# Layer 0's output products moved within the sixteen slots of a batch, with a ring of 14 attention outputs

## The reference

```
latent = x @ Wkv_down                      # (b, 512, 64)
q = x @ Wq                                 # 16 heads of 64
k, v = latent @ Wk_up, latent @ Wv_up      # 16 heads of 64
attn = softmax(causal(q k^T / 8))
x = layernorm(x + einsum(attn v, Wout))
...
```

## Time and profile before

| what | value |
|---|---|
| time, median of 3 runs | 1711.63 us (1711.25 to 1713.56) |
| profiled execution: own time | 1704.8 us |
| profiled execution: span | 1702.8 us |
| PE busy share of the span | 93% |
| DVE, ACT, POOL | 71%, 60%, 28% |
| mean granted clock of PE | 0.975 |
| last matmul of layer 0's attention ends | 763.5 us into the span |

### The profile page before, as it was taken

The page is one execution under the profiler, slowest core; times in us unless marked ns, Lnnn a source line. Parts: engine busy times, 40 slices in busy tenths (PEclk is TensorE's granted clock), DMA queues, the critical chain, the costliest instruction groups (busy, mean ns, idle before and its releaser), DMA issues. The chain is left out here.

```text
span 1702.8 us, 29270 instructions
## 1 busy us (share of the span) xinstructions
PE 1584.4 (93%) x9060; PEld 1102.6 (65%) x9060; DVE 1213.1 (71%) x4130; ACT 1016.8 (60%) x2544; POOL 470.8 (28%) x853
## 2 busy tenths in 40 slices
PE   7999999999999999987799977899999998899996
PEld 5667676767676766753588845666666655376765
DVE  4888878887888878755655546999999886134445
ACT  3876767676766767634444454677777766634340
POOL 4001001010101010100275467677786643100001
PEclk9999999999999999998899977999999999999998
DMA  5111111111121211103055628677686665000000
GB/s 165 38 48 45 40 38 38 50 44 48 40 50 38 52 43 38 38 7 100 12 170 163 140 68 113 88 111 106 103 118 87 95 86 98 1 7 25 13 25 31
DMA packets 72583, 111.67 MB, mean 66 GB/s; under 512 B 13265, under 2 KB 38321, under 8 KB 72305
## 3 DMA queue, kind: packets, MB, share of 16 engines
q1 hardware_dynamic: 61024, 81.04, 24.3%
q0 software_dynamic: 10016, 26.48, 6.9%
q10 hardware_dynamic: 1392, 2.29, 0.4%
HBM read 40.04 MB, written 18.87 MB: 35 GB/s over the span
## 5 line engine op out<-in xcount | busy, mean ns | idle before, releaser
L394 ACT ACTIVATE c_probs<-c_probs,a_negmax 128x128 f32<-128x128 f32 (+3 forms) x512 | 280.5, 553 | 0.0
L399 ACT ACTIVATE c_probs<-a_ps_trans 128x512 f32<-128x512 f32 (+1 forms) x256 | 125.0, 488 | 213.0 <-PE a_ps_trans L300 212.1
L1885 ACT ACTIVATE c_probs<-a_ps_st 128x384 f32<-128x384 f32 (+1 forms) x384 | 191.1, 529 | 90.2 <-PE a_ps_st L1685 88.7
L2038 DVE CUSTOM_DVE_ANT_0 a_junk<-a_ps_score,c_mask 128x128 f32<-128x128 f32 (+3 forms) x512 | 220.1, 487 | 33.5 <-PE a_ps_score L1663 30.4
L472 DVE CUSTOM_DVE_ANT_0 c_probs<-a_ps_score,c_mask 128x128 f32<-128x128 f32 (+3 forms) x512 | 219.6, 486 | 15.2 <-PE a_ps_score L281 14.1
L300 PE MATMUL a_ps_trans<-c_ident,c_probs 128*128 128x128 f32 x1280 | 188.0, 277 | 17.6 <-DVE c_probs L489 15.9
L300 PEld LDWEIGHTS a_ps_trans<-c_ident,c_probs 128*128 128x128 f32 x1280 | 146.4, 141 | 87.9 <-issue 39.3
L575 POOL TENSOR_SCALAR a_rstd<-a_mv 128x4 f32<-128x4 f32 x8 | 1.8, 231 | 689.3 <-DVE a_mv L502 689.3
L280 PE MATMUL a_ps_score<-a_kh,a_qs 128*128 128x128 f32 (+3 forms) x512 | 167.2, 350 | 1.3 <-issue 1.1
L489 DVE TENSOR_SCALAR c_probs<-c_probs,a_recip 128x128 f32<-128x128 f32 (+3 forms) x512 | 164.4, 386 | 4.5
L1685 PE MATMUL a_ps_st<-a_qs,a_ks 128*128 128x512 f32 (+3 forms) x512 | 149.7, 362 | 16.7 <-ACT c_probs L1885 8.6
(11 more groups left out here) (290 smaller groups left out, 3157.2 us busy)
## 6 DMA issues: line engine op xcount, KB each, us to landing
a_qs<-a_qlow SPq DMA_DIRECT2D x128, 128.0 KB, 2.2
slot_out<-m_y SPq DMA_DIRECT2D x80, 128.0 KB, 2.0
a_qs<-a_words_even SPq DMA_DIRECT2D x64, 128.0 KB, 4.1
a_ks<-a_words_even SPq DMA_DIRECT2D x64, 128.0 KB, 5.5
c_X<-in_x SPq DMA_DIRECT2D x8, 512.0 KB, 3.9
token_rows<-c_X SPq DMA_DIRECT2D x8, 512.0 KB, 5.7
a_qs<-a_counts SPq DMA_DIRECT2D x32, 128.0 KB, 4.3
a_qs<-a_hid SPq DMA_DIRECT2D x32, 128.0 KB, 4.7
```

The costliest lines, as they stand in the source:

```text
L394: act.activation(at, at, ACT.Exp, scale=-1.0, bias=negmax[:, n % 4, i:i + 1], accum_out=rowsum[:, n % 4, i:i + 1]).then_inc(s_exp, 1)
L399: act.activation(probT[:, n % 4, TGCOL[grp]:TGCOL[grp] + TGLEN[grp]], ps_trans[(3 * n + grp) % 2][:, 0:TGLEN[grp]], ACT.Copy).then_inc(s_p ...
L1885: act.activation(probT[:, r8, col:col + width], ps_st[item % 2][:, 0:width], ACT.Exp).then_inc(s_stc, 1)
L2038: dve.tensor_tensor_reduce(out=junk[:, to:to + keys], in0=ps_score[g][:, at:at + keys], in1=C.mask[:, L - keys:L], scale=-1.0, scalar=3.0e ...
```

## The change

The output products of a batch go from steps 20, 22, 24, 26 to steps 20, 24, 30, 32, their additions with them, and the batch's `write` from step 28 to 36. Modulo 16 the products are then in 4, 8, 14 and 0, and `write` in 4. Since the last product of a batch comes six slots later, the ring `yT` gets 14 entries for 12. Its two new entries hold, until pairs 12 and 13 are written, the small weights that had tensors of their own; the sum of the memory is the same. Because `latent` of a batch now falls between the second and the third product of the batch two before, the waits around `ps_kv` are set anew.

```diff
-NY = 12
+NY = 14
...
-        wdq, wuqT = S.sb("wdq", [P, P]), S.sb("wuqT", [P, P])
-        wdkv, wukT, wuvT = S.sb("wdkv", [P, 2, P]), S.sb("wukT", [P, 2, P]), S.sb("wuvT", [P, 2, HD])
-        wkr, wqr = S.sb("wkr", [64, P]), S.sb("wqr", [64, P])
+        wuvT = S.sb("wuvT", [P, 2, HD])
...
+        spare = yT[:, NY - 2:NY, :].rearrange("p r t -> p (r t)")
+        wdq, wuqT = spare[:, 0:P], spare[:, P:2 * P]
+        wdkv, wukT = (spare[:, 2 * P * j:2 * P * (j + 1)].rearrange("p (c d) -> p c d", d=P) for j in (1, 2))
+        wkr, wqr = spare[0:64, 6 * P:7 * P], spare[0:64, 7 * P:8 * P]
...
-        START, KEYS, VALUES, KEEP_VALUES, OUT, ADD, WRITE = 12, 13, 2, 3, (20, 22, 24, 26), (21, 23, 25, 27), 28
+        START, KEYS, VALUES, KEEP_VALUES, OUT, ADD, WRITE = 12, 13, 2, 3, (20, 24, 30, 32), (21, 25, 31, 33), 36
...
                 def latent(b):
...
                     if b >= 2:
-                        pe.wait_ge(s_sum, TT * (b - 1))
+                        pe.wait_ge(s_sum, TT * (b - 2) + 2)
...
                 def values(b):
                     pe.wait_ge(s_kl, b + 1)
+                    if b >= 2:
+                        pe.wait_ge(s_sum, TT * (b - 1))
...
                 def out(b, t):
...
                         if b or t:
                             pe.wait_ge(s_sum, TT * b + t)
+                        if t == 2:
+                            pe.wait_ge(s_kl, min(b + 3, B))
```

## The result

The changed kernel takes 1702.87 us (median of 6 runs, 1701.19 to 1706.0), the kernel before 1712.42 (6 runs beside them, 1711.25 to 1718.41). The ratio is 0.994 with a 95% interval of 0.9929 to 0.995: 9.6 us, or 0.6%, faster. The forecast was 1701.0.

What follows compares the result with a forecast made beforehand. PE, busy 528.8 of 540 us in layer 0's attention, with a gate-to-gate ring through ACT and DVE setting empty pairs. Savings 8.2 + 1.4 + 1.0 = 10.6 us, from the median 1711.6, give 1701.0; range 1695 to 1708.

Steps and rivals of the forecast that it cites:

- The products give nothing by being spread: Layer 0's attention, steady batches: four long and two empty pairs either way, so spreading gains 0.
- `write` leaves the ring, 6 x 1.37 and 1.36: Gate-to-gate chain through PE, ACT and DVE: removing `write` saves 8.2 us in latent pairs, 1.36 in slot 124.
- 0.4 to 0.6 us of cover in slot 4: Slot 4's product pair: with `write` there, DVE's normalisation still ends 0.4 to 0.6 us before PE's gate.
- Rival B: Slot 4 or a new wait: no cover, `write` costs what it did in slot 12; 1709.2 us, chance 0.09.
- The tail, net 1.0: Last but one batch: two emptied pairs save 5.8 us, two products put later cost 4.8; net gain 1.0.
- New waits, weights and POOL: nothing: Attention stage: waits for latent, keys, values and outputs, small-weight loads and POOL's moved work all cost nothing.
- Rival C: Slot 2: the queries' low words land late beside weight loads, losing 17.9 us; 1718.9 us, chance 0.06.
- Rival A: Empty pairs between long ones run at PE's own pace, up to 5.6 us more; 1695.4 us, chance 0.08.
- Rival D: Later stages: PE's clock rises or falls at other places; 1701 +- 7 us, chance 0.09 beyond the forecast's own range.
- The sum for the attention: Attention stage: 8.2 and 1.4 from `write` plus 1.0 from the tail make 10.6 us saved.
- The range given for the forecast alone: Whole kernel: 1697 to 1704 us, from a tail of -3 to +4 about its term; chance 0.68.
- the signs: Profile after: latent pair 10.9, product pairs 12.4, empty 9.48, period 90.3, waits some 6, last product 10 to 11 earlier.

Runs made afterwards that it cites:

- write_only: The kernel before with only `write` moved, from step 28 to step 36, products left unspread; 1703.42 us, ratio 0.995 to the kernel before.
- two_and_two: The changed kernel with its products in two adjacent couples, steps 20, 22, 30 and 32, instead of spread; 1703.29 us, ratio 0.9948 to the kernel before.
- write_at_34: The changed kernel with `write` at step 34, a pair without an output product, instead of 36; 1710.25 us, ratio 0.9985 to the kernel before.
- cover5: The changed kernel with five more small DVE operations behind `write` in slot 4 of six batches; 1704.58 us in a single run.
- after_again: The changed kernel run once more without further edits, on one chip beside the kernel before; 1702.61 us, ratio 0.9948.
- the halves: The changed kernel with each batch's first two products cut in halves, in steps 20, 22, 24 and 26; 1698.3 us, ratio 0.9916 to the kernel before.
- ring_only: The kernel before with the 14-entry `yT` and the small weights in it, but its own schedule and waits; median 1712.74 us, ratio 0.9993.

## Why the prediction was right

By its own steps:

- *The products give nothing by being spread.* Right: write_only has the period without spreading, two_and_two has it with other distances, write_at_34 has spreading without the gain.
- *`write` leaves the ring, 6 x 1.37 and 1.36.* Right: 12.27 became 10.90, and slot 124's pair 712.70 - 703.23 = 9.47 for 10.84. Batch 0 of the trace before had shown the pair without `write` already.
- *0.4 to 0.6 us of cover in slot 4.* Right: 0.55 by the trace, 0.50 by cover5. Rival B's loss didn't occur, but there was little room: 1.13 us more of DVE's work, less than `write` itself, already cost 0.63 in cover5. One detail was wrong and harmless: from the last product to `write` it is 4 slots now (32 to 36) for 2 before, not the same number.
- *The tail, net 1.0.* The mechanism was right and the size too small: 1.5 to 1.7. A product cost 2.2 us there where I had reckoned (6.8 - 2.0) / 2 = 2.4, and an empty pair saved 2.95 for 2.89.
- *New waits, weights and POOL: nothing.* Right as far as the traces show: between 40 and 760 us PE waits nowhere for `a_qs` or `ps_kv` and, except for ACT's last copy as before (0.69 us), nowhere for the entries of `yT`. The low words land in 2.2 us, between 40 and 700 us in at most 3.2 (3.6 in after_again, and 4.0 in the kernel before). Rival C's collision didn't occur in slot 2: there POOL's issues end at 288.50, their loads land in some 3 us, and the low words leave at 294.2 and 294.9. A run that forces it wasn't made.
- *Rival A.* The empty pairs became 0.05 us shorter behind long ones, not 0.5. What A had hoped for needed another edit, the halves.
- *Rival D.* From the first matmul behind the attention to the end of the span it is 938.0 to 940.8 us in ten traces, 939.5 in the changed kernel and 938.7 in ring_only; the shift didn't move the later stages by more than their scatter. The trace of before alone has 929.9.

The sum for the attention was 10.6 us; from the gate of slot 4 of batch 0 on it is 732.63 - 720.97 = 11.7. The 1.1 us more are the tail (0.6) and pairs that are a few hundredths shorter. The timed runs show 9.6 us, and the interval of their ratio stands for 8.6 to 12.2, so they can't tell the two apart. The range given for the forecast alone has a slip: a net tail of -3 to +4 about its term of 1.0 makes 1698 to 1705, not 1697 to 1704; the time lies in either.

Of the signs, the first product of the last batch starts at 737.09, where the kernel before has

```profile
749.39 3.72 PE L342 MATMUL a_ps_kv<-a_wvo,a_yT 128*128 128x256 f32 x16 [0.70 <-ACT a_yT L413]
```

That is 12.3 us earlier, outside the 10 to 11 that were named; 0.6 of it is the earlier gate of slot 4 of batch 0 (39.64 for 40.28), the rest the 11.7. The other signs came: a period of 90.2, waits of 5.1 us, no empty pair under 9.3, slot 4 at 12.42.

The two profiled executions differ by only 1704.8 - 1701.9 = 2.9 us, and whoever compares them alone misses most of the gain. It isn't lost in the attention. It lies in the expert stage, which the change leaves alone: the transposes of its inputs, first and last start, before and in ring_only:

```profile
L1072 PE MATMUL m_ps_zT<-c_ident,m_z x160: 272/273/476, 847.5 to 977.0; 128*128 128x128 f32 x160
```

```profile
L1074 PE MATMUL m_ps_zT<-c_ident,m_z x160: 272/273/473, 847.3 to 985.4; 128*128 128x128 f32 x160
```

That is 129.5 us in the profile of before and 138.1 in that of ring_only, whose gates are the same; the nine other traces have 137.5 to 138.7. The profiled execution of before was shorter by 8 to 9 us in this stage. That accounts for its 6.8 us under the median of the runs, while those of the other kernels that ran more than once lie within 1.5 us of theirs. Against the profiled execution of ring_only, whose expert stage has the usual length, that of the changed kernel is 1712.97 - 1701.93 = 11.0 us shorter. What kept the prediction right was that it took its sum from the median. It didn't know why the two differed: from the profiled execution it would have said 1694.2, outside its own range of 1695 to 1708.

## What to carry to other kernels

Where engines pass work round in a ring, price an operation by the ring and not by its engine's busy share: DVE was 83% busy in this stage, and 1.39 us of it still stood in full on the path in seven pairs of slots, while the same operations were free in a pair where PE had 3 us more to do. Look for a stretch of the same trace in which the operation is absent (here batch 0); it gives the price without a model. And where the gaps that remain are shorter than a block of filling work, cut the block rather than shift it, but count what follows its end as well.

## What was not expected of the hardware

The expert stage, which no edit touches, has two lengths in the eleven traces, 129.5 us once and 137.5 to 138.7 ten times. In windows of the same stretch, PE is busy all through in the short one, and not in a long one (ring_only): length, then busy times of PE, PEld, DVE, ACT, POOL, then granted clock, DMA share and GB/s; first the short one.

```profile
855.00:865.00 10.00, 10.00 (x56) 8.20 (x55) 7.60 (x23) 3.93 (x13) 7.87 (x8) 1.00 0.63 172
865.00:875.00 10.00, 10.00 (x56) 8.32 (x55) 5.14 (x19) 4.10 (x13) 7.56 (x9) 1.00 0.63 185
```

```profile
855.00:865.00 10.00, 4.59 (x19) 2.98 (x18) 2.92 (x9) 1.12 (x5) 5.87 (x8) 0.85 0.41 109
865.00:875.00 10.00, 10.00 (x46) 8.17 (x45) 5.73 (x18) 3.14 (x10) 5.32 (x5) 0.81 0.43 133
```

In the long one PE is idle for half of the first 10 us, and its granted clock is lower there and in the next 10 us (0.85 and 0.81 for 1.00). What holds it up at the start of the stage wasn't looked into and stays open.
